# Rows of x to columns through a scratch in HBM and VectorE's 32x32 blocks, with f units in front of o units

## The chip, the cores and the metric

One Trainium2 chip (trn2), one core of it. The metric is the device time of one execution in microseconds, as the median of several runs; a profiled execution of the same kernel is taken beside them.

## The reference, cut to what matters

x and ctx are 32 batches of 256 rows of 512 numbers, all float32. Each batch gets a causal attention with 16 heads of 32 numbers, whose queries come from the normalised rows of x and whose keys and values come from ctx, and then a linear layer on rows quantised to a grid of 6-bit numbers.

```python
x = x + tanh(g_xattn[0]) * xattn(layernorm(x), ctx, ctx, w_q, b_q, w_k, b_k, w_v, b_v, w_o, b_o)
x = x + tanh(g_ffn[0]) * ffn(layernorm(x), weight, bias)
```

## The kernel before, in words

**Tiling.** Every product runs over columns that must lie on partitions, so rows of x, of ctx and of the quantised input have to be turned. Numbers are split in a high and a low part of type float32r, and a product is three matmuls (`three`, L546: hi by hi, hi by lo, lo by hi). A batch is two halves of 128 rows. Work comes in units: cT, xT and dT are turns of a half (rows of context, of normalised x, of the quantised rows), q and k are projections of a half of the heads, v, o and f of a half of the rows. q, k, v, o, f have four parts of three or six matmuls each, cT, xT and dT one part of four transposes. A unit takes one of four banks (`proj`) in turn.

**Steps and slots.** The program has 36 steps of 16 slots. Step i works at once on several batches: the context of batch i is loaded and turned; q half 0, k and v are of batch i-1; q half 1, the 16 heads' scores, maxima, exponentials and divisions are of batch i-2; o is of batch i-3 and f of batch i-4. One slot holds one head: TensorE makes its scores (L605, L606), turns the probabilities of the head three slots back (`transpose_probs`, L616, which waits for `div_ok`, the division by GpSimd), weighs values in slots 3 and 11 (L632), and then makes the parts of units that UNITS and SLOT_PARTS give to the slot. The scores of head h wait until VectorE has the maxima of head h-2 (`max_ok`).

**The engines.** Each engine runs its own program in order. VectorE per slot: maxima of the head (`maxima`, L891), reciprocal of the one before (L949), then what a unit finished in the slot before needs (`unit`: L920 for q_lo and k_lo, L943 for the low part of a turned half, L929 and L905 for o, L937 for f), a copy of the turned probabilities in every second slot (L1028), then xn (`normal_rows`, L1008, slots 1 and 3), oT_lo (L954), the steps of the quantisation (L966, L972, L979), the turns of context (`turn`, L998, slots 5 and 8), and the moments of x (slot 14). ScalarE: `unit` (q_hi and k_hi L758, aT_hi L772, vs L750), oT_hi, copies, exponentials (L735), cT_hi (L783). GpSimd: cT_lo (L498), divisions (L458), add of biases, powers, scaling.

**How rows are turned before.** Context (but for batch 0) is loaded in four DMAs of one quadrant of 32 partitions each into c_quads (`context`, L370) so that VectorE's 32x32 block transposes finish the turn in SBUF (cols); ScalarE and GpSimd split it. The normalised rows xn are turned by TensorE: 4 transposes a half (L660, kind xT), then ScalarE (L772) and VectorE (L943) read the bank.

**The DMA queue.** All DMAs are issued by SyncE (SP), in the order of its `step` (L389 to L435). A stack (`stack`, L374 to L382) is 12 DMAs that copy q_hi, q_lo, q_hi or k_hi, k_hi, k_lo of half the heads into q_stack or k_stack. The order of a step i is: k stack of pair 1 of batch i-2; loads of context i; load of x of batch i; q stack of pair 1 of batch i-2; stores of batch i-4; k stack of pair 0 of batch i-1; q stack of pair 0 of batch i-1 (waits for q_lo, `left["q"]`). There is one k_hi for all batches, so the first k unit of a batch may write it only when the last stack of k of the batch before has landed:

```python
                    if some(n := b + half):
                        for e in range(2):
                            act.wait_ge(stacked[kind][1 - half][e], STACK_DMAS * 16 * n)
```

In the first steps, at the start, TensorE turns the identity 12 times (WAKING, L543) before the context of batch 0 (L660) and the first weight (L582, `transpose_weight`).

Of the kernel before, what the change touches and what calls it, by code (L numbers as in the profile page):

```python
# [24 lines left out]
F32 = mybir.dt.float32  # L25
# [7 lines left out]
P = 128  # L33
# [32 lines left out]
WEIGHT_SLOTS = {"k": (1, (0, 0, 0, 0)), "q": (1, (4, 4, 4, 4)), "v": (1, (6, 9, 9, 9)), "o": (1, (10, 12, 12, 13)),  # L66
# [6 lines left out]
XB_SLOTS = (5, 6)  # L73
LN1_SLOT = SLOTS - 2
XN_SLOTS = (1, 3)
QUAD = 32
TURN_SLOTS = (5, 8)
TURN_SLOTS_1 = (12, 13)
# [4 lines left out]
def fused_kernel(nc, x, ctx_in, g_xattn, g_ffn, w_q, b_q, w_k, b_k, w_v, b_v, w_o, b_o, w_f, b_f, out):  # L83
# [16 lines left out]

    usual = [(u, part) for u, (kind, _, _) in enumerate(UNITS) for part in range(PARTS[kind])]
    slot_of = [s for s in range(SLOTS) for _ in range(SLOT_PARTS[s])]
    assert len(usual) == len(slot_of)
    lag_of = {(kind, half): lag for kind, half, lag in UNITS}
# [3 lines left out]
    for i in range(STEPS):  # L108
        if i == B + 2:

            for s, (kind, half) in LAST_O:
                work.setdefault((i, s), []).extend((kind, half, i - lag_of[kind, half], p) for p in range(PARTS[kind]))
        else:
            for (u, part), s in zip(usual, slot_of):
                kind, half, lag = UNITS[u]
                if live(i - lag):
                    work.setdefault((i, s), []).append((kind, half, i - lag, part))

    work[1, 0] = [("cT", half, 0, 0) for half in range(T)] + work.get((1, 0), [])

# [13 lines left out]
    def some(n):  # L134

        return not isinstance(n, int) or n > 0

    with ExitStack() as es:
# [29 lines left out]
        xn = sb("xn", [P, T, D])  # L168
        aT_hi = sb("aT_hi", [P, KC, S], F32R)
# [83 lines left out]
        turned = sem("turned")  # L253
# [64 lines left out]
        def turn_slots(b):  # L318

            return TURN_SLOTS_1 if b == 1 else TURN_SLOTS if b > 1 else ()  # L320
# [19 lines left out]
        def _(sp):  # L340
# [26 lines left out]
            def context(b):  # L367

                for g in range(NQ):
                    sp.dma_start(c_quads[g * QUAD:(g + 1) * QUAD, :, :],  # L370
                                 ctx_in[b, :, g * P:(g + 1) * P].rearrange("(n l) d -> l n d", l=QUAD)).then_inc(
                                     c_in, 16)
# [11 lines left out]
            def step(i, ph):  # L384
                if live(i - 2):

                    if some(n := HEADS * (i - 2)):

                        sp.wait_ge(max_ok, n)  # L389
                    sp.wait_ge(left["k"], 2 * (i - 2) + 2)  # L390
                    stack("k", i - 2, 1)
                if at(i, 0):
                    load_first()
                elif live(i):

                    if i == 1:
                        sp.wait_ge(done["cT"], 2)
                    else:  # L400
                        sp.wait_ge(turned, 2 * (i - 1))
                    context(i)

                    if i == 1:
# [18 lines left out]
                b = i - 1  # L423
                if live(b):
                    if some(b):


                        sp.wait_ge(max_ok, HEADS * (b - 1) + HEADS // 2)
                    else:

                        sp.wait_ge(left["k"], 2 * b + 1)
# [10 lines left out]
        def _(pool):  # L442
# [57 lines left out]

            def step(i, ph):
# [9 lines left out]
                for s in range(SLOTS):  # L511

                    for t, turn_slot in enumerate(turn_slots(i)):
                        if s == turn_slot + 2 and live(i):
                            context_lo(i, t)
                    lag, h = (2, s - 1) if s else (3, SLOTS - 1)
# [10 lines left out]
                    if i == 0 and s == LN1_SLOT + 1:  # L527
                        deviation_in(0)
                    if s == 0 and i > 1 and live(i - 1):
                        deviation_in(i - 1)  # L530
# [8 lines left out]
        def _(pe):  # L539
# [3 lines left out]
            for _ in range(WAKING):  # L543
# [20 lines left out]
            def transpose_weight(u, w, c):  # L564

                if w == "f" and c == 0:

                    pe.wait_ge(wd_ok, 1)
                elif w in "kv" and c == 0:
# [3 lines left out]
                elif w in "qo" and c % 2 == 0:  # L573
# [6 lines left out]
                cols = slice(c, D, KC) if w in "kv" else slice(c * P, (c + 1) * P)  # L580
# [58 lines left out]
            def unit(kind, half, b, part):  # L639
# [7 lines left out]
                if kind in ("xT", "cT", "dT"):  # L647
# [10 lines left out]
                    for c in range(KC):  # L658
                        cols = slice(c, D, KC) if kind == "cT" else slice(c * P, (c + 1) * P)
# [52 lines left out]
        def _(act):  # L712
# [27 lines left out]
            def unit(kind, half, b):  # L740
# [20 lines left out]
                else:  # L761
                    dst = cT_hi[:, 0] if kind == "cT" else aT_hi
                    if kind == "cT":
                        pass
                    elif kind == "xT":

                        if some(n := 2 * (b - 3) + half + 1):
                            act.wait_ge(done["f"], n)
                    else:
# [6 lines left out]
            def context_hi(b, t):  # L776

                act.wait_ge(turned, 2 * (b - 1) + t + 1)
                if some(n := 2 * (b - 1)):
# [4 lines left out]
                                     ACT.Copy).then_inc(hi_ok["cT"], 1)  # L784

# [17 lines left out]
            def step(i, ph):  # L803
                for s in range(SLOTS):
# [16 lines left out]
                    for t, turn_slot in enumerate(turn_slots(i)):  # L821
                        if s == turn_slot + 1 and live(i):
                            context_hi(i, t)
                    for chunk in weight_chunks(i, s - 1):
# [15 lines left out]
        def _(dve):  # L840
# [146 lines left out]
            def moments_in(b):  # L987

                dve.wait_ge(x_in, 16 * (b + 1))
                moments(b + 1, (0, 1), xs[:, b % X_RING], stats1, mom1, var1, st1, mo1, va1)  # L990

            def turn(b, t):

                dve.wait_ge(c_in, 16 + 16 * NQ * b)
                if b > 1:

                    dve.wait_ge(left["cT"], 2 * (b - 1) + t + 1)
                nc.vector.transpose(cols[:, t, :, :].rearrange("p c (n l) -> p n c l", l=QUAD),  # L998
                                    c_quads[:, t * NQ:(t + 1) * NQ, :].rearrange("p n (e c) -> p n c e",
                                                                                c=KC)).then_inc(turned, 1)  # L1000

            def normal_rows(b, t):

                dve.wait_ge(rs1, b + 1)
                if some(n := 2 * b):

                    dve.wait_ge(done["xT"], n)
# [3 lines left out]
            def step(i, ph):  # L1011
                for s in range(SLOTS):
# [16 lines left out]
                    if s in XN_SLOTS and i > 1 and live(i - 1):  # L1029
                        normal_rows(i - 1, XN_SLOTS.index(s))  # L1030
# [7 lines left out]
                    for t, turn_slot in enumerate(turn_slots(i)):  # L1038
                        if s == turn_slot and live(i):
                            turn(i, t)  # L1040
# [8 lines left out]
                    if s == LN1_SLOT and i > 1 and live(i):  # L1049
                        moments_in(i)  # L1050
                    if i == 1 and s == 1:
                        moments_in(0)
# [28 lines left out]
```

## Time and profile before

| what | value |
|---|---|
| median of 3 runs | 1389.93 us (1389.61 to 1392.1) |
| the profiled execution's own time | 1392.38 us |
| its span, first to last instruction | 1390.6 us |
| mean granted TensorE clock | 0.989 of full speed |
| TensorE matmuls busy | 1354.2 us, 97% |
| VectorE | 1124.7 us, 81% |
| ScalarE | 916.6 us, 66% |
| GpSimd | 938.7 us, 68% |
| DMA | 159.10 MB, 114 GB/s on average |

Busy time is the time in which an instruction runs; matmuls overlap in the pipeline, so that what one costs is the distance of its start from the next one's start and not its duration. The same holds, by 0.1 us or so, for VectorE. A row of the timeline begins with its start in us, then its duration (of all, where it ends with a count over x1), engine, line, operation, output and inputs; brackets at its end hold the idle time in front of it and what ended it.

### The profile page before, as it was taken

How to read it: one execution, taken by the hardware profiler on the slowest of the kernel's cores; microseconds unless marked ns; L12 is line 12 of the kernel's file. 1: busy time of each engine (PE TensorE's matmuls, PEld its weight loads, DVE VectorE, ACT ScalarE, POOL GpSimd, SP SyncE). 2: the span in 40 equal slices, each digit the busy share in tenths (PEclk: the TensorE clock that was granted, in tenths of full speed). 3: DMA queues.
4: the chain of work that ended last, by engine and by line, in shares of the span. 5: the costliest groups of instructions: out<-in, count | busy, mean ns of one | idle time of the engine just before them, and what ended most of it. 6: DMA issues, size and time to landing. Idle time of an engine off the chain costs nothing.

```text
span 1390.6 us, 34895 instructions
## 1 busy us (share of the span) xinstructions
PE 1354.2 (97%) x10608; PEld 1198.5 (86%) x10608; DVE 1124.7 (81%) x4219; ACT 916.6 (66%) x2969; POOL 938.7 (68%) x1449
## 2 busy tenths in 40 slices
PE   7899999999999999999999999999999999999987
PEld 7788888898888888888888888888888889889865
DVE  5768888788888888888878878888888888888773
ACT  4667666667666666667666667666666666766661
POOL 1657776677676777676677676677677667767564
PEclk9999999999999999999999999999999999999998
DMA  8444344444444444434444434444444444443320
GB/s 253 118 112 107 103 111 124 118 129 107 109 109 120 124 128 117 107 101 119 121 126 123 108 99 115 126 119 124 110 106 109 126 118 128 110 116 99 88 62 31
DMA packets 181912, 159.10 MB, mean 114 GB/s; under 512 B 30176, under 2 KB 164320, under 8 KB 181728
## 3 DMA queue, kind: packets, MB, share of 16 engines
q1 hardware_dynamic: 181728, 156.88, 43.3%
q8 instruction: 87, 1.43, 0.5%
q14 instruction: 97, 0.79, 0.2%
HBM read 39.33 MB, written 16.78 MB: 40 GB/s over the span
## 4 chain that ended last, share of the span: by engine, by line
PE 59%; DVE 20%; SPq 9%; issue 5%; DMA 3%; ACT 1%; POOL 1%; DVEq 0%; ACTq 0%; POOLq 0%
PE proj L549 14%; PE proj L551 13%; PE proj L550 13%; SPq L380 9%; PE pT_ps L616 8%; DVE all_probs L891 5%; PE proj L632 3%; DMA k_stack<-k_lo 3%; DVE stats L899 3%; PE s_ps L605 3%; PE proj L660 2%; DVE all_probs L1028 2%; DVE k_lo L920 2%; PE s_ps L606 1%; DVE oT_lo L954 1%
## 5 line engine op out<-in xcount | busy, mean ns | idle before, releaser
L458 POOL TENSOR_TENSOR all_probs<-all_probs,rden 128x128 f32<-128x128 f32 (+1 forms) x1024 | 504.1, 514 | 347.5 <-DVE rden L949 346.5
L735 ACT ACTIVATE all_probs<-all_probs,neg_max 128x128 f32<-128x128 f32 (+1 forms) x1024 | 458.3, 449 | 242.4 <-DVE neg_max L891 242.2
L891 DVE CUSTOM_DVE_ANT_0 all_probs<-s_ps,causal 128x128 f32<-128x128 f32 (+1 forms) x1024 | 324.4, 354 | 144.2 <-PE s_ps L606 137.1
L616 PE MATMUL pT_ps<-ident,all_probs 128*128 128x128 f32 x1536 | 265.0, 282 | 9.9 <-POOL all_probs L458 7.2
L735 ACT ACTIVATION_READ_ACCUMULATOR all_probs<-all_probs,neg_max 128x1 f32 x1024 | 193.1, 189 | 0.0
L817 ACT ACTIVATE all_probs<-pT_ps 128x384 f32<-128x384 f32 x256 | 125.4, 490 | 87.4 <-PE pT_ps L616 87.2
L616 PEld LDWEIGHTS pT_ps<-ident,all_probs 128*128 128x128 f32 x1536 | 160.8, 142 | 25.2 <-issue 14.1
L549 PE MATMUL proj<-cT_hi,wk_hi 128*128 128x256 f32 x512 | 153.8, 300 | 1.4 <-DVE wk_lo L844 1.4
L605 PE MATMUL s_ps<-k_stack,q_stack 96*128 96x256 f32 x512 | 152.8, 299 | 2.1 <-DVE neg_max L891 2.0
L549 PE MATMUL proj<-aT_hi,wq_hi 128*128 128x256 f32 x512 | 151.0, 295 | 2.3 <-DVE aT_lo L943 2.3
L550 PE MATMUL proj<-cT_lo,wk_hi 128*128 128x256 f32 x512 | 142.7, 279 | 0.0
L551 PE MATMUL proj<-cT_hi,wk_lo 128*128 128x256 f32 x512 | 142.5, 278 | 0.0
L550 PE MATMUL proj<-aT_lo,wq_hi 128*128 128x256 f32 x512 | 142.4, 278 | 0.0
L551 PE MATMUL proj<-aT_hi,wq_lo 128*128 128x256 f32 x512 | 142.4, 278 | 0.0
L1028 DVE COPY all_probs<-pT_ps 128x384 f32<-128x384 f32 x256 | 139.7, 546 | 2.1 <-PE pT_ps L616 1.9
L549 PE MATMUL proj<-wf_hi,aT_hi 128*128 128x512 f32 x256 | 111.9, 437 | 6.6 <-DVE oT_lo L954 5.8
L606 PE MATMUL s_ps<-k_stack,q_stack 96*128 96x128 f32 x512 | 116.1, 227 | 0.0
L549 PE MATMUL proj<-wo_hi,oT_hi 128*128 128x512 f32 x260 | 110.9, 426 | 0.9 <-DVE oT_lo L954 0.9
L758 ACT ACTIVATE k_hi<-proj,bias_k 128x256 fp32r<-128x256 f32 x128 | 53.0, 464 | 85.6 <-DMA k_stack<-k_lo 81.0
L605 PEld LDWEIGHTS s_ps<-k_stack,q_stack 96*128 96x128 f32 x512 | 96.9, 189 | 14.3 <-DVE neg_max L891 3.3
L549 PE MATMUL proj<-wv_hi,cT_hi 128*128 128x512 f32 x256 | 108.3, 423 | 0.0
L606 PEld LDWEIGHTS s_ps<-k_stack,q_stack 96*128 96x128 f32 x512 | 98.2, 192 | 10.5
(119 smaller groups left out, 3607.9 us busy)
## 6 DMA issues: line engine op xcount, KB each, us to landing
k_stack<-k_hi SPq DMA_DIRECT2D x512, 64.0 KB, 2.0
q_stack<-q_hi SPq DMA_DIRECT2D x512, 64.0 KB, 2.1
xs_yz<-in_x SPq DMA_DIRECT2D x32, 512.0 KB, 5.2
k_stack<-k_lo SPq DMA_DIRECT2D x256, 64.0 KB, 2.0
q_stack<-q_lo SPq DMA_DIRECT2D x256, 64.0 KB, 2.1
out<-xs_yz SPq DMA_DIRECT2D x64, 256.0 KB, 2.3
c_quads<-in_ctx SPq DMA_DIRECT2D x124, 128.0 KB, 2.9
vs<-in_L_xattn_w_k SPq DMA_DIRECT2D x2, 512.0 KB, 5.8
```

Source lines behind the costliest of these rows:

```text
L380: sp.dma_start(dst[r * DK:(r + 1) * DK, h:h + GROUP + 1:GROUP, :].bitcast(F32), src[j * DK:(j + 1) * DK, :, :].bitcast(F32)).then_inc(stac ...
L458: last = nc.gpsimd.tensor_tensor(p, p, rden[:, sd, t, h:h + 1].to_broadcast([P, (1 + t) * P]), ALU.mult)
L549: nc.tensor.matmul(out, a_hi(c), b_hi(c), start=c == 0, stop=False)
L550: nc.tensor.matmul(out, a_hi(c), b_lo(c), start=False, stop=False)
L551: last = nc.tensor.matmul(out, a_lo(c), b_hi(c), start=False, stop=c == KC - 1)
L605: nc.tensor.matmul(bank[:, P:3 * P], q_stack[:, h, P:S], k_stack[:, h, :], start=True, stop=True)
L606: nc.tensor.matmul(bank[:, 0:P], q_stack[:, h, 0:P], k_stack[:, h, 0:P], start=True, stop=True).then_inc(s_done, 1)
L616: last = nc.tensor.transpose(pT_ps[h % 2][:, m * P:(m + 1) * P], probs[:, h % P_RING, m * P:(m + 1) * P], ident[:, :])
L735: last = nc.scalar.activation(probs[:, h % P_RING, cols], probs[:, h % P_RING, cols], ACT.Exp, scale=-1.0, bias=neg_max[:, sd, t, h:h + 1] ...
L817: nc.scalar.activation(probsT[:, h % AV_HEADS, :], pT_ps[1][:, 0:3 * P], ACT.Copy).then_inc(pT_odd, 1)
L891: last = nc.vector.tensor_tensor_reduce(probs[:, h % P_RING, cols], s_ps[h % 2][:, cols], causal[:, (1 - t) * P:], 1.0, MASKED, ALU.add, A ...
L1028: nc.vector.tensor_copy(probsT[:, h % AV_HEADS, :], pT_ps[0][:, 0:3 * P]).then_inc(pT_even, 1)
```

## The change

xT leaves TensorE for all batches but the first. The normalised rows xn (now made in slot 14 of step i for batch i, after moments in slots 7 and 9 and the power in slot 11) are written to a scratch in HBM, xn_rows, by one DMA (`rows_out`), and read back by four DMAs in quadrants (`rows_back`) into the same place in SBUF. VectorE turns them in 32x32 blocks in slots 5 and 6 into cols, halves swapped, ScalarE makes aT_hi and GpSimd aT_lo (`rows_hi`, `rows_lo`). The turns of context move to slots 0 and 1 and their loads to the end of the step before. The order of parts is written out in SLOT_WORK: f comes in front of o, and q half 0 ends in slot 12 (before: slot 10). The weight of q is turned with the stride c, D, KC like k and v. The identity is turned another 16 times before the first weight.

```diff
-UNITS = [("q", 1, 2), ("dT", 0, 4), ("k", 0, 1), ("dT", 1, 4), ("f", 0, 4), ("xT", 0, 1), ("f", 1, 4), ("xT", 1, 1),
-         ("o", 0, 3), ("o", 1, 3), ("q", 0, 1), ("v", 0, 1), ("k", 1, 1), ("v", 1, 1)]
-SLOT_PARTS = (3, 3, 3, 1, 3, 4, 3, 3, 3, 3, 3, 1, 3, 3, 3, 2)
+SLOT_WORK = ("q1 q1 q1", "dT0 q1 k0", "k0 k0 k0", "dT1", "f0 f0 f0", "f0 f1 f1", "f1 f1 o0", "o0 o0 o0", "o1 o1 o1",
+             "o1 v0 v0", "v0 v0", "q0", "q0 q0 q0", "k1 k1 k1", "k1 v1 v1", "v1 v1")
-WAKING = 12
+WAKING = (12, 16)
-XB_SLOTS = (5, 6)
-LN1_SLOT = SLOTS - 2
-XN_SLOTS = (1, 3)
+XB_SLOTS = (4, 5)
+LN1_SLOTS = (7, 9)
+RSTD_SLOT = 11
+XN_SLOT = 14
-TURN_SLOTS = (5, 8)
-TURN_SLOTS_1 = (12, 13)
+C_TURNS, C_TURNS_1, C_TURNS_2 = (0, 1), (12, 13), (2, 3)
+X_TURNS = (5, 6)
...
     work[1, 0] = [("cT", half, 0, 0) for half in range(T)] + work.get((1, 0), [])
+    work[1, 5] = [("xT", half, 0, 0) for half in range(T)] + work.get((1, 5), [])
+    xn_rows = nc.dram_tensor("xn_rows", [S, D], F32, kind="Internal").ap()
+        xn_quads = xn[:, :, :].rearrange("p t (n d) -> p (t n) d", d=P)
...
+            def rows_out(b):
+                sp.wait_ge(xn_ok, T * (b + 1))
+                sp.dma_start(xn_rows.rearrange("(t p) d -> p t d", p=P), xn[:, :, :]).then_inc(xn_out, 16)
+
+            def rows_back(b):
+                sp.wait_ge(xn_out, 16 * b)
+                for quadrant, rows in quarters(xn_rows):
+                    sp.dma_start(xn_quads[quadrant, :, :], rows).then_inc(xq_in, 16)
...
             def step(i, ph):
+                if i > 1 and live(i - 1):
+                    rows_out(i - 1)
                 if live(i - 2):
...
                     sp.wait_ge(left["k"], 2 * (i - 2) + 2)
                     stack("k", i - 2, 1)
...
                     sp.dma_start(xs[:, place(ph, 0), :, :], batch_of(x, i)).then_inc(x_in, 16)
+                if i > 1 and live(i - 1):
+                    rows_back(i - 1)
                 if live(i - 2):
...
                     stack("q", i - 2, 1)
+                b = i - 1
+                if live(b):
+                    if some(b):
+                        sp.wait_ge(max_ok, HEADS * (b - 1) + HEADS // 2)
+                    sp.wait_ge(left["k"], 2 * b + 1)
+                    stack("k", b, 0)
                 if live(i - 4):
...
                 if live(b):
-                    stack("k", b, 0)
                     sp.wait_ge(left["q"], 2 * b + 1)
                     stack("q", b, 0)
+                if i > 0 and live(i + 1):
+                    context(i + 1)
...
+            def rows_lo(b, t):
+                pool.wait_ge(hi_ok["xT"], 2 * b + t + 1)
+                tok = slice(t * P, (t + 1) * P)
+                nc.gpsimd.tensor_tensor(aT_lo[:, :, tok], cols[:, 1 - t, :, :], aT_hi[:, :, tok].bitcast(F32),
+                                        ALU.subtract).then_inc(left["xT"], 1)
...
+            def turn_rows(b, t):
+                dve.wait_ge(xq_in, 16 * NQ * b)
+                if live(b + 1):
+                    dve.wait_ge(left["cT"], T * (b + 1) + T - t)
+                else:
+                    dve.wait_ge(left["xT"], T * (b - 1) + t + 1)
+                turn(xn_quads, t, 1 - t, x_turned)
```

## Rows read from the trace of the kernel before

**Rows 1.** Windows view, 600 to 641.3: stretch, length, busy time by engine, clock, DMA

```profile
600.00:641.30 41.30, 41.30 (x332) 36.78 (x331) 35.18 (x132) 28.56 (x95) 29.54 (x47) 1.00 0.44 117
```

**Rows 2.** Timeline of the SyncE queue, three stretches: start, duration, what is issued

```profile
162.11 1.22 SPq L380 DMA_DIRECT2D k_stack<-k_hi  x2
...
616.49 1.23 SPq L380 DMA_DIRECT2D k_stack<-k_hi  x2
...
624.16 2.08 SPq L370 DMA_DIRECT2D c_quads<-in_ctx  x4
626.28 0.45 SPq L412 DMA_DIRECT2D xs_yz<-in_x  x1
627.07 0.59 SPq L380 DMA_DIRECT2D q_stack<-q_hi  x1
...
635.43 1.18 SPq L421 DMA_DIRECT2D out<-xs_yz  x2
...
1236.86 1.23 SPq L380 DMA_DIRECT2D k_stack<-k_hi  x2
```

**Rows 3.** Waits view, whole span: us in total, times, longest

```profile
ACT k_hi L758 <- DMA k_stack<-k_lo: 81.0, 30, 3.4
```

**Rows 4.** Timeline of ScalarE, the first k unit of a step

```profile
625.61 0.84 ACT L758 ACTIVATE k_hi<-proj,bias_k 128x256 fp32r<-128x256 f32 x2 [1.95 <-DMA k_stack<-k_lo]
```

**Rows 5.** VectorE: timeline, end of q half 0; waits view, 625.6 to 647.8

```profile
646.55 0.85 DVE L920 SCALAR_TENSOR_TENSOR q_lo<-proj,bias_q,q_hi 128x256 fp32r<-128x256 f32 x2
...
DVE all_probs L891 <- PE s_ps L606: 1.9, 4, 0.9
```

**Rows 6.** Timeline of TensorE around one xT unit

```profile
629.98 0.39 PE L551 MATMUL proj<-wf_hi,aT_lo 128*128 128x512 f32 x1
630.21 0.60 PE L660 MATMUL proj<-ident,xn 128*128 128x128 f32 x4
...
630.88 0.39 PE L550 MATMUL proj<-wf_lo,aT_hi 128*128 128x512 f32 x1
```

**Rows 7.** Groups by line and form: busy us, mean ns; idle before, releaser

```profile
L943 DVE TENSOR_TENSOR aT_lo<-proj,aT_hi 128x512 fp32r<-128x512 f32 x128 | 86.8, 678 | 5.6 <-ACT aT_hi L772 5.6
...
L998 DVE STREAM_TRANSPOSE cols<-c_quads 128x512 f32<-128x512 f32 x62 | 68.0, 1098 | 0.0
...
L498 POOL TENSOR_TENSOR cT_lo<-cols,cT_hi 128x512 fp32r<-128x512 f32 x62 | 81.0, 1307 | 0.5 <-ACT cT_hi L783 0.5
```

**Rows 8.** Timeline of VectorE: starts, from which spacings are taken

```profile
606.81 0.67 DVE L972 TENSOR_REDUCE amax<-xs_yz 128x16 f32<-128x512 f32 x1
607.40 0.53 DVE L966 TENSOR_SCALAR xs_yz<-xs_yz,mom,rstd 128x512 f32<-128x512 f32 x1
...
611.09 0.54 DVE L1028 COPY all_probs<-pT_ps 128x384 f32<-128x384 f32 x1
611.54 0.17 DVE L979 TENSOR_SCALAR blk<-amax 128x16 f32<-128x16 f32 x1
...
612.33 0.29 DVE L891 CUSTOM_DVE_ANT_0 all_probs<-s_ps,causal 128x128 f32<-128x128 f32 x1
...
612.97 1.27 DVE L899 BATCH_NORM_STATS2 stats<-xs_yz 128x6 f32<-128x512 f32 x2
...
614.62 0.17 DVE L909 TENSOR_SCALAR var<-mom 128x2 f32<-128x2 f32 x1
```

**Rows 9.** Timeline of GpSimd: the division of head 3

```profile
629.00 0.97 POOL L458 TENSOR_TENSOR all_probs<-all_probs,rden 128x128 f32<-128x128 f32 x2 [2.85 <-DVE rden L949]
```

**Rows 10.** Timeline of TensorE: scores of two slots in a row

```profile
606.61 0.28 PE L605 MATMUL s_ps<-k_stack,q_stack 96*128 96x256 f32 x1
...
609.22 0.28 PE L605 MATMUL s_ps<-k_stack,q_stack 96*128 96x256 f32 x1
```

**Rows 11.** Timeline of TensorE at the start: the first weight's transposes

```profile
8.64 1.95 PE L582 MATMUL s_ps<-ident,vs 128*128 128x128 f32 x8 [2.13 <-DMA vs<-in_L_xattn_w_k]
```

**Rows 12.** Windows view, 60 to 64, columns as in rows 1

```profile
60.00:64.00 4.00, 1.34 (x8) 1.20 (x7) 3.55 (x14) 2.86 (x12) 3.99 (x7) 0.79 0.38 95
```

More of the change, by code:

```diff
@@ L99, in live @@
         return not isinstance(b, int) or 0 <= b < B
[L101 to L104, printed above, removed]
+    usual = [(s, (name[:-1], int(name[-1]))) for s in range(SLOTS) for name in SLOT_WORK[s].split()]
+    assert all(sum(unit == u for _, u in usual) == PARTS[unit[0]] for unit in LAGS)
     work = {}
@@ L111, in fused_kernel @@
             for s, (kind, half) in LAST_O:
-                work.setdefault((i, s), []).extend((kind, half, i - lag_of[kind, half], p) for p in range(PARTS[kind]))
+                work.setdefault((i, s), []).extend((kind, half, i - LAGS[kind, half], p) for p in range(PARTS[kind]))
         else:
[L114 to L117, printed above, removed]
+            part_of = dict.fromkeys(LAGS, 0)
+            for s, unit in usual:
+                if live(i - LAGS[unit]):
+                    work.setdefault((i, s), []).append((*unit, i - LAGS[unit], part_of[unit]))
+                part_of[unit] += 1
     work[1, 0] = [("cT", half, 0, 0) for half in range(T)] + work.get((1, 0), [])
+    work[1, 5] = [("xT", half, 0, 0) for half in range(T)] + work.get((1, 5), [])
     taken = []
@@ L398, in step @@
                     if i == 1:
[L399 to L404, printed above, removed]
+                        context(1)
                         sp.wait_ge(xn_ok, 2)
@@ L541, in _ @@
             pe.wait_ge(ident_ok, 1)
-            for _ in range(WAKING):
+            for _ in range(WAKING[0]):
                 nc.tensor.transpose(proj[BANKS - 1][:, 0:P], ident[:, :], ident[:, :])
@@ L762, in unit @@
                     dst = cT_hi[:, 0] if kind == "cT" else aT_hi
[L763 to L769, printed above, removed]
+                    if kind == "dT":
                         act.wait_ge(done["q"], 2 * (min(b + 2, B - 1) if isinstance(b, int) else b + 2) + 2)
@@ L985, in scales, with moments_in @@
                                         ALU.mult).then_inc(inv_ok, 1)
-            def moments_in(b):
+            def moments_in(b, t):
                 dve.wait_ge(x_in, 16 * (b + 1))
-                moments(b + 1, (0, 1), xs[:, b % X_RING], stats1, mom1, var1, st1, mo1, va1)
-            def turn(b, t):
-                dve.wait_ge(c_in, 16 + 16 * NQ * b)
[L995 to L1000, printed above, removed]
+                nc.vector.bn_stats(stats1[:, t, :], xs[:, b % X_RING, t, :]).then_inc(st1, 1)
+                if t == T - 1:
+                    dve.wait_ge(st1, T * (b + 1))
+                    for n in range(T):
+                        last = nc.vector.bn_aggr(mom1[:, n, :], stats1[:, n, :])
+                    last.then_inc(mo1, 1)
+                    dve.wait_ge(mo1, b + 1)
+                    nc.vector.tensor_scalar(var1[:, :], mom1[:, :, 1], LN_EPS, None, ALU.add).then_inc(va1, 1)
@@ new lines, in turn, with turn_context @@
+            def turn(quads, t, place, turned):
+                nc.vector.transpose(cols[:, place, :, :].rearrange("p c (n l) -> p n c l", l=QUAD),
+                                    quads[:, t * NQ:(t + 1) * NQ, :].rearrange("p n (e c) -> p n c e",
+                                                                              c=KC)).then_inc(turned, 1)
+            def turn_context(b, t):
+                dve.wait_ge(c_in, 16 + 16 * NQ * b)
+                if b > 2:
+                    dve.wait_ge(left["xT"], T * (b - 2) + T - t)
+                elif b == 2:
+                    dve.wait_ge(left["cT"], T * (b - 1) + t + 1)
+                turn(c_quads, t, t, c_turned)
@@ L1028, in step @@
                         nc.vector.tensor_copy(probsT[:, h % AV_HEADS, :], pT_ps[0][:, 0:3 * P]).then_inc(pT_even, 1)
-                    if s in XN_SLOTS and i > 1 and live(i - 1):
-                        normal_rows(i - 1, XN_SLOTS.index(s))
+                    if s == XN_SLOT and i > 0 and live(i):
+                        for t in range(T):
+                            normal_rows(i, t)
                     for r in range(2):
```

96 lines of the change are left out of this document (61 added, 35 removed).

## The prediction

> **What bounds the kernel now.** I read the windows view first. In the stretch [rows 1] TensorE is busy 41.30 of 41.30 us at full granted clock, VectorE 35.18, GpSimd 29.54, ScalarE 28.56: TensorE sets the time. A step takes 41.34 us: between the first and the last of these SyncE rows, 26 steps apart, lie 1074.75 us [rows 2]. The other thing to see is in the same group: SyncE's own queue. A stack of q or k rows is 12 DMAs, and the next item of the queue starts 7.67 us (616.49 to 624.16) or 8.36 us (627.07 to 635.43) later. Four stacks, four loads of context, one of x and two stores are some 36 us of issue in 41.34. What hangs on that queue stands in the waits view [rows 3]: ScalarE waits 30 times, 81.0 us in all, to overwrite k_hi until the k stack of the batch before has landed, and by the code SyncE's q stack waits for q_lo in turn. So beside TensorE there is a ring, once per step. Call K the start of k_hi for k half 0 (625.61, 1.5 us after the last of the k stack's DMAs left SyncE [rows 4]) and Q the end of q_lo for q half 0 (646.55 plus 0.85, 647.40 [rows 5]). From K to Q are 21.8 us of VectorE, TensorE and ScalarE; from Q to the next K SyncE issues two stacks. Two fast stacks are 15.3 us and the landing 1.5, so today's ring has up to 41.3 - 21.8 - 15.3 - 1.5 = 2.7 us of slack, and TensorE stays full.
>
> **The change, part by part.**
>
> *TensorE, less work.* A unit of four transposes sits between two matmuls: from 629.98 to 630.88 are 0.90 us where two matmul spacings of 0.23 would be 0.46 [rows 6]. 0.44 us a unit, two units a step, 31 steps: 27.3 us, all on today's bound. TensorE alone would take 40.46 a step.
>
> *VectorE.* Off: two subtractions of 678 ns; on: two 32x32 turns of 1098 ns [rows 7], 0.84 us a step more, 36.0 of 40.5. Not a bound by its sum. ScalarE reads cols where it read a bank: nothing counted, it is busy 28.56 of 41.30. GpSimd gains two subtractions like cT_lo's, 1307 ns [rows 7], 32.2 of 40.5; hidden by its idle time, and I place them behind divisions that TensorE wants only later.
>
> *SyncE.* On: one store of 512 KB to the scratch, which I take at 0.5 us of issue (the 512 KB load of x takes 0.45 [rows 2]; between 0.4 and 1.1), and four loads shaped like the context's, 2.1 us. The sum becomes 38.7. But what counts is where things now stand: q half 0 is finished by TensorE in slot 12, not slot 10; then come its stack, the four context loads (formerly behind the k stack), the new store, and only then the k stack whose landing ScalarE waits for at slot 3. The loads of context, now issued from Q+7.7 on, land about 11.5 after Q, and VectorE's first turn of context (slot 0) waits for them some 5 us; it still reaches slot 3 at about Q+17.7, ahead of k_lo at Q+21, so that wait is covered by the ring, for as long as the ring is this long. The wait of rows_back for the store is covered: the k stack lies between. The wait for max_ok before the k stack of pair 0 also finds slack, since SyncE then waits for Q anyway.
>
> *The ring after the change, Q to K.* Stack of q 8.0 (mean of 7.67 and 8.36), context 2.1, store 0.5, stack of k 8.0, landing 1.5: 20.1 us, with 19.4 to 22 as ends (every issue fast; both slow and a landing 1 us longer).
>
> *The ring, K to Q.* Of the 21.8 us before, VectorE idles 1.9 in front of scores [rows 5], so 19.9 are work. The stretch now ends in slot 13 instead of 11. It gains, in spacings of starts [rows 8]: two pairs of maxima with reciprocal at 0.64, a copy of probabilities 0.45, both block maxima 1.18, a second normalise 0.46 (as long as the copy), one scales 0.79, the moments of x 1.8, oT_lo of the other half 0.59 (an instruction of the block maximum's 0.67 us). It loses one xn (0.46, moved to slot 14) and the two subtractions (1.18). Both turns were in it already. Together plus 4.9: 24.8 us of VectorE without a pause. TensorE's way through the same stretch: head 3 is divided 4.36 us after K (629.00 and 0.97 [rows 9]), 3.9 without the xn in front, so slot 6 starts at K+3.7; from there to slot 13 are five full slots of 2.6 us (606.61 to 609.22 [rows 10]), one of 1.9 and one of 2.8, so 17.7, then maxima and q_lo 1.7: 23.1. VectorE's 24.8 is the later one.
>
> *Sum per step.* 24.8 + 20.1 = 44.9, plus 0.4 for the clock (below): 45.3 us, 3.96 more than 41.34. TensorE's 0.88 us saving buys nothing, for it is no longer the bound: it will wait in slot 6 for the division of head 3, which waits for ScalarE's k_hi.
>
> *Sum over the kernel.* 27 steps (4 to 30) at 3.96 are 106.9. Steps 31 and 32 have no context load left to issue, so 1.8 each, 3.7. Steps 2 and 3 lack the o or f work and are slower than TensorE's sum already; I give them 4 together. The tail stays.
>
> *Start.* 16 turns of the identity before the first weight. Today TensorE idles 2.13 us until the weight lands at 8.64, and eight transposes take 1.95 us with their tail, at the lower clock [rows 11]. Sixteen take 3.4 us, so the weight's transposes begin 1.1 us later; if the clock is then up (2.4 instead of 1.2 GHz), the 40 instructions behind cost half, some 3 us less. Between -3 and +1; I take -1.5.
>
> Total: +106.9 + 3.7 + 4 - 1.5 = +113. The profiled execution took 1392.4 us (span 1390.6), 2.5 above the median of 1389.9; so 1505 against that execution and 1503 against the median.
>
> **A rule weighed here.** The rows say that a DMA's issue occupies SyncE for about 0.64 us in a stretch of 12, and that an engine ends up waiting for the last of them. The Trainium skill, "DMA: Bandwidth & Descriptors", "Issuing engines are not separate DMA queues", says that the sequencer's time to start a DMA is usually small against the DMA itself. By that rule the order on SyncE would be almost free, and the sum would be the first rival's. The trace disagrees for DMAs of this size: 0.64 us of issue each, against 1.5 us from the end of the last issue to its landing.
>
> **Rivals.**
>
> *1. Faster: the queue does not bind and TensorE's saving comes through.* The mechanism is 62 units fewer on an engine that has no idle time: 1389.9 - 27.3 - 1.5 = 1361. It decides if the ring takes less than 40.5 us, 4.4 below my sum; for that, SyncE would have to issue stacks in some 6 us instead of 8, or k_hi would have to be free without its landing. For it: TensorE has no idle time in the stretch now. Against it: even the fast ends, 23.1 and 19.4, make 42.5. Chance 0.10, and 0.02 that the two effects cancel.
>
> *2. The ring with TensorE's way as its middle part.* If VectorE's 24.8 is overcounted, 23.1 + 19.5 = 42.6 a step, 1.3 more than before: 27 x 1.3, and -0.5 each in steps 31 and 32, +3 for steps 2 and 3, -1.5: about 1425. Chance 0.15.
>
> *3. The ring and the clock.* Once TensorE waits some 2 us at slot 0 (first half of the q stack lands 5.4 after Q, three us late) and again at slot 6, the clock may fall each time. In the stretch 60 to 64, with TensorE busy 1.34 of 4 us, the mean granted clock is 0.79 [rows 12], partly at 1.2 GHz. Seven us at half clock cost 3.5: TensorE's way becomes 26.6 and overtakes VectorE's 24.8. With 20.1 to 21 for the rest, 47.2 a step: 27 x 5.9 + 8 + 5 - 1.5 = +171, 1561. Against it: the gaps are short, and full work follows. The Trainium skill, "TensorE: Matmul & The Clock Gate", "HAM oscillation", describes a loop whose waits for DMAs let the clock fall in every pass, which is this case's pattern; whether 2 us are enough, no row here shows for a full step. Chance 0.18; its milder half is the 0.4 us in my sum.
>
> *4. The rows come back late.* rows_back is issued behind 512 KB of x. If it lands after K+5.0, where VectorE's slot 5 asks for it, each us of lateness is a us of the ring. It is at about that point; 0 to 1 us, inside the range.
>
> **The numbers.** Forecast (44 to 46.5 a step) 0.55, rival 3 0.18, rival 2 0.15, faster 0.10, no change 0.02. The time is that of the likeliest, 1503. The range reaches from rival 2 to rival 3, 1425 to 1560, and leaves out the faster case and the far end of the clock. A measurement here tells 0.2% from no change. Faster 0.10, same 0.02, slower 0.88.
>
> **What the changed profile would show.** The four transposes of xn only in step 1; TensorE's share falls from 97% to about 90, with idle time in front of the probabilities' transposes released by GpSimd. ScalarE still waits at k_hi for k_stack, some 3 us or more each, and VectorE's wait for the loads of context in slot 0 is new. SyncE waits for q_lo some 5 us or more a step and never for k_lo; the k stack of pair 1 starts some 10.6 us after q_lo. VectorE has no pause from k_lo in slot 3 to q_lo in slot 13. The clock after each gap tells rival 3. The forecast is wrong if ScalarE no longer waits at k_hi, or if a step takes 40.5 us with TensorE full.

## The result: 1595.4 us, 14.8% slower

The changed kernel takes 1595.4 us (median of 4 runs, 1591.38 to 1598.6) beside 1390.6 us for the kernel before on the same chip: ratio 1.1477, 95% interval [1.1459, 1.1495]. The direction was forecast; the time was not, since 1595 lies above the range of 1425 to 1560. The profiled execution's span is 1594.2 us against 1390.6.

The head of the profile of after: TensorE's share fell from 97% to 88%.

```profile
span 1594.2 us, 34649 instructions
...
PE 1408.2 (88%) x10376; PEld 1223.1 (77%) x10376; DVE 1143.3 (72%) x4219; ACT 913.5 (57%) x2969; POOL 1011.9 (63%) x1511
...
PE 50%; SPq 21%; DVE 10%; issue 10%; DMA 7%; POOL 1%; ACT 0%; DVEq 0%; POOLq 0%; ACTq 0%
SPq L404 17%; PE proj L581 10%; PE proj L582 10%; PE proj L583 10%; PE pT_ps L652 8%; PE proj L668 7%; DMA c_quads<-in_ctx 5%; SPq L387 3%; DVE all_probs L936 3%; PE s_ps L641 2%; DVE q_lo L965 2%; PE proj L696 2%; DVE all_probs L1099 1%; PE s_ps L642 1%; DMA xn<-xn_rows 1%
```

The last two lines are the chain that ended last. SyncE's queue (SPq), which an engine-by-engine sum never shows, holds a fifth of it; 17% of 1594 us is 271 us, 9 per step, which is one stack and a little. A chain that went through two stacks a step, as the forecast's ring does, would hold nearly twice that. The transfers in it are those of context, not those of k_stack.

The waits view of after, us in total, times, longest, agrees (the third line answers to [rows 3]):

```profile
DVE cols L1048 <- DMA c_quads<-in_ctx: 180.8, 29, 7.2
...
PE proj L668 <- issue: 80.5, 32, 2.7
...
ACT k_hi L794 <- DMA k_stack<-k_lo: 52.3, 30, 6.2
```

ScalarE waits less for the k stack than before (52.3 against 81.0 us), and VectorE waits for the loads of context in 29 steps, 6.2 us each. The windows view of one step of after, columns as in [rows 1]:

```profile
600.00:647.30 47.30, 42.54 (x321) 37.04 (x320) 35.29 (x135) 28.01 (x93) 32.22 (x48) 0.93 0.49 125
```

VectorE has nearly the 35.2 us of before and TensorE 42.54 us, in a step of 47.3: no engine is a bound by its sum.

**Where the time went.** SyncE issues the store to xn_rows once a step, 31 times, the first at 60.2 and the last at 1480.2: 47.33 us a step, 5.99 more than the 41.34 of before. The first k stack of step 2 is issued at 60.72 where before it was at 40.45: 20.3 us at the start. The same stack of step 32 follows at 1480.84 where before it was at 1278.52, so the 30 steps between cost 182.0 us (a little over 30 x 5.99, as the first steps of before are shorter than 41.34). The remaining 1.3 of the 203.6 us of span lie in the last steps.

**One steady step.** The chain through it, in order of time: start, duration, what.

```profile
615.67 0.40 DVE q_lo L965
616.09 0.59 SPq L404
...
623.12 0.60 SPq L404
623.76 1.52 SPq L387
...
626.31 2.93 DMA c_quads<-in_ctx
629.33 0.32 issue
...
630.95 0.46 DVE all_probs L1099
631.41 2.68 issue
634.10 2.79 PE proj L668 x32
636.88 0.83 PE pT_ps L652 x3
...
663.44 0.59 SPq L404
```

It begins and ends with the same event, SyncE's first issue of the q stack after q half 0 is done. q_lo ends at 616.07 (Q). SyncE issues 12 DMAs of the stack until 623.72 and four of context until 626.76, the last lands at 629.24 (626.31 plus 2.93): 13.2 after Q. Only then can VectorE go on, and the timeline of the three other engines shows who stands behind it:

```profile
629.26 1.08 DVE L1048 STREAM_TRANSPOSE cols<-c_quads 128x512 f32<-128x512 f32 x1 [6.54 <-DMA c_quads<-in_ctx]
...
630.91 0.40 ACT L771 ACTIVATE all_probs<-all_probs,neg_max 128x128 f32<-128x128 f32 x1 [7.24 <-DVE neg_max L936]
...
634.10 2.79 PE L668 MATMUL proj<-all_probs,vs 128*32 128x256 f32 x32 [2.72 <-issue]
...
636.91 0.84 ACT L794 ACTIVATE k_hi<-proj,bias_k 128x256 fp32r<-128x256 f32 x2 [1.53 <-DMA k_stack<-k_lo]
...
637.79 0.88 DVE L965 SCALAR_TENSOR_TENSOR k_lo<-proj,bias_k,k_hi 128x256 fp32r<-128x256 f32 x2 [2.63 <-ACT k_hi L794]
```

The turn of context stands in VectorE's slot 0, in front of the maxima of head 1. ScalarE's exponential of head 1 waits 7.24 us for those, and behind it in ScalarE's program are cT_hi, aT_hi, q_hi and then the copy of the last head's turned probabilities of the batch before (L858, at 633.51). TensorE needs that copy for the values in slot 3 (L668), which start at 634.10, as the copy ends; the profile has only "issue" for this wait, and the time of the copy is what names it. From there TensorE has no gap until it has made q half 0 in slot 12; q_lo ends at 663.42. So: Q to landing 13.2, landing to values 4.8, values to the next Q 29.3: 47.3 us. k_hi starts at 636.91, after TensorE is already running again, and holds nobody up but VectorE for 2.63 us.

### The profile page after: what moved, and what is told of

It reads as the page before. It is cut to its first block, busy times and chain, and to the rows that moved or that the text cites. A ratio compares the mean times of both kernels' runs of the same rounds, so it can differ in the third digit from the quotient of the medians.

```text
span 1594.2 us, 34649 instructions
## 1 busy us (share of the span) xinstructions
PE 1408.2 (88%) x10376; PEld 1223.1 (77%) x10376; DVE 1143.3 (72%) x4219; ACT 913.5 (57%) x2969; POOL 1011.9 (63%) x1511
## 4 chain that ended last, share of the span: by engine, by line
PE 50%; SPq 21%; DVE 10%; issue 10%; DMA 7%; POOL 1%; ACT 0%; DVEq 0%; POOLq 0%; ACTq 0%
SPq L404 17%; PE proj L581 10%; PE proj L582 10%; PE proj L583 10%; PE pT_ps L652 8%; PE proj L668 7%; DMA c_quads<-in_ctx 5%; SPq L387 3%; DVE all_probs L936 3%; PE s_ps L641 2%; DVE q_lo L965 2%; PE proj L696 2%; DVE all_probs L1099 1%; PE s_ps L642 1%; DMA xn<-xn_rows 1%
## 5 line engine op out<-in xcount | busy, mean ns | idle before, releaser
L652 PE MATMUL pT_ps<-ident,all_probs 128*128 128x128 f32 x1536 | 281.8, 296 | 17.0 <-POOL all_probs L479 10.2
L641 PE MATMUL s_ps<-k_stack,q_stack 96*128 96x256 f32 x512 | 161.8, 316 | 56.1 <-DVE neg_max L936 43.8
L668 PE MATMUL proj<-all_probs,vs 128*32 128x256 f32 (+1 forms) x2048 | 134.8, 421 | 80.5 <-issue 80.5
L652 PEld LDWEIGHTS pT_ps<-ident,all_probs 128*128 128x128 f32 x1536 | 170.3, 149 | 38.1 <-issue 24.8
L1048 DVE STREAM_TRANSPOSE cols<-c_quads 128x512 f32<-128x512 f32 x62 | 67.7, 1091 | 180.8 <-DMA c_quads<-in_ctx 180.8
L858 ACT ACTIVATE all_probs<-pT_ps 128x384 f32<-128x384 f32 x256 | 125.1, 489 | 103.5 <-PE pT_ps L652 102.9
L668 PEld LDWEIGHTS proj<-all_probs,vs 128*32 128x32 f32 x2048 | 77.6, 137 | 122.6 <-issue 108.6
L641 PEld LDWEIGHTS s_ps<-k_stack,q_stack 96*128 96x128 f32 x512 | 101.0, 197 | 86.6 <-DVE neg_max L936 50.6
L581 PE MATMUL proj<-aT_hi,wq_hi 128*128 128x256 f32 x512 | 153.5, 300 | 0.0
L581 PE MATMUL proj<-cT_hi,wk_hi 128*128 128x256 f32 x512 | 150.4, 294 | 1.8 <-DVE wk_lo L889 1.8
L965 DVE SCALAR_TENSOR_TENSOR k_lo<-proj,bias_k,k_hi 128x256 fp32r<-128x256 f32 x128 | 55.4, 474 | 83.5 <-ACT k_hi L794 83.5
```

The source lines that it names most:

```text
L581: nc.tensor.matmul(out, a_hi(c), b_hi(c), start=c == 0, stop=False)
L641: nc.tensor.matmul(bank[:, P:3 * P], q_stack[:, h, P:S], k_stack[:, h, :], start=True, stop=True)
L652: last = nc.tensor.transpose(pT_ps[h % 2][:, m * P:(m + 1) * P], probs[:, h % P_RING, m * P:(m + 1) * P], ident[:, :])
L668: last = nc.tensor.matmul(bank[j * DK:(j + 1) * DK, half * S + kt * P:(half + 1) * S], vs[:, sd, kt, d:d + DK], probsT[:, GROUP * half + j ...
```

## Experiments

Step lengths below are taken as above, from the first and the last of the 31 issues of the store to xn_rows. Diffs are against the changed kernel unless said otherwise. Theory A is the context ring just read. Its rivals name something else: SyncE's order as such, the ring over k_hi, the clock.

### ctx_early: context in front of the q stack

```diff
+                if i > 1 and live(i + 1):
+                    context(i + 1)
                 if live(b):
                     sp.wait_ge(left["q"], 2 * b + 1)
                     stack("q", b, 0)
-                if i > 0 and live(i + 1):
+                if i == 1:
                     context(i + 1)
```

> The changed kernel with the loads of context i+1 issued by SyncE in front of the q stack of pair 0 (from step 2 on), not behind it. Theory A (the context ring): the step of 47.3 us is set by q_lo, q stack 7.7, context loads and their landing 5.5, VectorE's first context turn (waited 6.5 us), ScalarE's copy of head 15 behind it, and TensorE's values in slot 3. Then the wait at the context turn goes, and what is left is the ring over the k stack: 17.9 us from q_lo to k_hi and 24.8 of VectorE, 42.8 a step with the clock full again, so 27 steps less by 4.5, some 120 us: about 1473. Theory B (the k stack's ring as predicted, with the clock as its excess): only the 2.1 us of issue leave the ring, 1595 - 58 = about 1535, and ScalarE's wait at k_hi stays.

1514.87 us, ratio 1.0884 [1.0826, 1.0942]; span 1509.6, 44.41 a step (stores from 61.7 to 1394.1). The wait for context is gone from the waits view, and the one of the forecast's ring has taken its place:

```profile
ACT k_hi L796 <- DMA k_stack<-k_lo: 149.6, 31, 6.6
...
PE pT_ps L654 <- DVE all_probs L1101: 77.9, 31, 4.4
```

In one step of its timeline (ScalarE, TensorE, VectorE) Q is at 629.20 and the next at 673.46:

```profile
647.78 0.84 ACT L796 ACTIVATE k_hi<-proj,bias_k 128x256 fp32r<-128x256 f32 x2 [4.61 <-DMA k_stack<-k_lo]
...
650.15 0.52 PE L654 MATMUL pT_ps<-ident,all_probs 128*128 128x128 f32 x3 [2.23 <-DVE all_probs L1101]
...
653.88 1.11 DVE L1050 STREAM_TRANSPOSE cols<-xn 128x512 f32<-128x512 f32 x1 [0.98 <-DMA xn<-xn_rows]
```

Q to K is 18.6 (the forecast's 20.1 without 2.1 of context is 18.0), K to Q 25.7 (forecast 24.8, plus the late rows of rival 4: 0.98). So the forecast's ring exists and is about as long as forecast, but it is the second one. The gain is 2.9 us a step and not A's 4.5, since A's figure had this ring too short. The time alone decides nothing: it lies 42 us above A's and 20 us below B's. The waits do, and they are A's.

### turn_late: the turn of context two slots later

```diff
-C_TURNS, C_TURNS_1, C_TURNS_2 = (0, 1), (12, 13), (2, 3)
+C_TURNS, C_TURNS_1, C_TURNS_2 = (2, 3), (12, 13), (2, 3)
```

> The changed kernel with one edit: VectorE turns the context in slots 2 and 3 of every step instead of 0 and 1. SyncE's order and the work of every engine stay. Theory A (the step of 47.33 us is the ring q_lo, q stack, landing of the context loads, VectorE's turn of context in slot 0, ScalarE's exponential and copy behind it, values in slot 3, q half 0 in slot 12): the wait moves behind two more heads, some 5 us, and mostly goes; the ring over k_hi is next, about 44.4 us a step as with the context loads early, perhaps 1 us more because the turn of xn in slot 5 then waits for GpSimd's low part of context. 44.4 to 45.5 a step, about 1505 to 1540 us. Theory B (the late landing or SyncE's order itself holds the step, whoever waits for it): no gain, 1585 to 1605 us.

1619.1 us, ratio 1.1649 [1.163, 1.1669]; span 1616.3, 47.97 a step. That is a miss for A's number, and it isn't B either, by the timeline of a step (VectorE, then ScalarE, then TensorE):

```profile
642.20 1.16 DVE L1048 STREAM_TRANSPOSE cols<-c_quads 128x512 f32<-128x512 f32 x1 [0.27 <-DMA c_quads<-in_ctx]
...
657.00 1.11 DVE L1048 STREAM_TRANSPOSE cols<-xn 128x512 f32<-128x512 f32 x1 [1.37 <-POOL cT_lo L519]
...
649.52 0.84 ACT L794 ACTIVATE k_hi<-proj,bias_k 128x256 fp32r<-128x256 f32 x2 [8.02 <-DMA k_stack<-k_lo]
...
651.88 0.87 PE L652 MATMUL pT_ps<-ident,all_probs 128*128 128x128 f32 x3 [4.50 <-DVE all_probs L1099]
```

The wait for context is 0.27 us: that ring is open. The ring over k_hi closes instead, with 8.02 us of waiting: Q (628.75) to K 20.8, K to the next Q (676.70) 27.2. Against ctx_early each part is longer for a reason in the rows: in Q to K the four context loads, 3.19 us in this step, still stand in front of the k stack; in K to Q, TensorE starts again after a gap of 4.50 us at half clock (windows view, 652 to 656, the column behind the busy times):

```profile
652.00:656.00 4.00, 3.93 (x11) 2.75 (x12) 3.63 (x14) 3.47 (x12) 3.67 (x5) 0.50 1.01 187
```

Nearly 4 us at half clock are 2 us of work lost; K to Q is 1.5 us longer than in ctx_early. The two rings of the changed kernel are thus almost equal, and opening one alone leaves the step to the other.

### qfirst_only: q half 0 two slots earlier

```diff
-             "o1 v0 v0", "v0 v0", "q0", "q0 q0 q0", ...
+             "o1 q0 q0", "q0 q0", "v0", "v0 v0 v0", ...
```

> The changed kernel with one edit: the parts of q half 0 in slots 9 and 10 in front of v half 0. Loads of context stay behind the q stack, the moments of batch 1 stay early. Theory A (both rings start at q_lo, so that its slot decides): in steps of 40.5 us q_lo now ends some 10.3 us before slot 0 instead of 5, the loads of context land 13.2 after it, VectorE's first context turn waits 2 us instead of 6.5, and the copy of head 15 comes just in time: 40.5 to 41.5 a step, and with the start unchanged 1385 to 1420. Theory B: the place of the loads behind the stack costs by itself, 43 us a step or more, over 1450.

1442.04 us, ratio 1.0381 [1.0337, 1.0426]; span 1440.7, 42.44 a step (53.2 to 1326.5). This edit touches neither SyncE's order nor a wait; it shortens what both rings have in common. By one step of the timeline (SyncE, VectorE, TensorE, and VectorE again), Q is at 639.49:

```profile
647.71 2.09 SPq L387 DMA_DIRECT2D c_quads<-in_ctx  x4
...
652.27 1.11 DVE L1048 STREAM_TRANSPOSE cols<-c_quads 128x512 f32<-128x512 f32 x1 [2.71 <-DMA c_quads<-in_ctx]
...
657.14 1.51 PE L668 MATMUL proj<-all_probs,vs 128*32 128x256 f32 x32 [0.93 <-issue]
...
680.26 0.86 DVE L965 SCALAR_TENSOR_TENSOR q_lo<-proj,bias_q,q_hi 128x256 fp32r<-128x256 f32 x2
```

Q to turn 12.8, turn to values 4.9, values to the next Q 24.0, where it was 29.3 (41.6 in this step; the mean is 42.44). The two slots left out were 5.4 us of TensorE in after (scores of slots 11 and 13, 655.80 and 661.18), and at a clock of 1.00 behind the values 1.3 more are gone; VectorE gives 1.6 of it back, since q_lo now comes 3.0 us behind TensorE's scores of its slot (677.24) and not 1.4. The ring is still the limit, 2 us above TensorE's 40.5, which is why A's 1420 was missed by 22 us. Of the 153.5 us of span gained, 147 are steps (30 times 4.89) and 7 the start, where q half 0 of step 1 is earlier too.

### ctx_qfirst and ctx_mom_qfirst: the edits together

ctx_qfirst has the two edits above, context in front of the q stack and q half 0 earlier:

> The changed kernel with two edits: the context loads in front of the q stack, and q half 0 in slots 9 and 10; the moments of batch 1 stay in slots 7 and 9 of step 1. Theory A (both rings fall below TensorE's sum, and the start is a price of its own): a step of 40.5 as with all three edits, and a start about 11 us later than there (the first store of rows at 53.2 instead of 41.8): 1383 to 1390 us. Theory B (the moments also hold back every step, or the start's price is hidden behind the rings): 1372 or over 1400 us.

1383.97 us, ratio 0.996 [0.9944, 0.9976]; stores from 53.7 to 1267.3, 40.45 a step. A's numbers, 40.5 and 1383 to 1390, hold. ctx_mom_qfirst adds the later moments of the next section:

> Both edits (context loads in front of the q stack; moments of batch 1 in slot 11 of step 1) and the parts of q half 0 in slots 9 and 10 in front of v half 0, so that q_lo comes two slots earlier. Theory A (two rings, nothing else): q_lo to k_hi stays 17.9 us and k_hi to q_lo falls from 24.8 to about 21 us, 39 a step, below TensorE's own 40.5: TensorE is the bound again without the 62 units, about 1390 - 27 = 1363, and no more than 1375. Theory B: the rows come back from the scratch too late, or SyncE's own sum (38.7 of 40.5 us) keeps it from this: 42 a step or more, over 1420.

1372.98 us, ratio 0.9865 [0.9836, 0.9893]; 40.53 a step, first store at 41.8, and in the windows view of 600 to 900 TensorE has 299.39 busy us of 300 at clock 1.00. Repeated as best_again:

> The version with the three edits once more, for an interval beside the other two: 1373, some 18 us below the kernel before, and 40.5 us a step. If the earlier time was chance, it lies above 1380.

1372.17 us, ratio 0.9875 [0.9821, 0.9928]. So this version takes 1.3% less than the kernel before, a small gain, but with the 95% interval below 1 in both runs, and 14% less than the changed one. The mechanism is that of the forecast's first rival, reached with other orders: a step of 40.5 where TensorE alone was to take 40.46. Its 1361 isn't reached: the first k stack of step 2 is issued at 43.92, 3.5 us later than before and not 1.5 earlier, and the 30 steps behind it save 22 us where the forecast has 27 in 31 steps (before, these 30 have 41.27 us on average).

### mom_late: the start

```diff
-                    if s in LN1_SLOTS and i > 0 and live(i):
+                    if s in LN1_SLOTS and i > 1 and live(i):
                         moments_in(i, LN1_SLOTS.index(s))
+                    if i == 1 and s == RSTD_SLOT:
+                        for t in range(T):
+                            moments_in(1, t)
```

> The changed kernel with the moments of x of batch 1 taken in slot 11 of step 1, not in slots 7 and 9; all other steps as they are. Theory A: TensorE's gap of 20 us at the start comes from VectorE, which waits 10.1 us in slot 7 of step 1 for x of batch 1 while the parts of the v weight are due behind it; then the first k stack of step 2 starts near 43 instead of 60.7 us and the time falls by 12 to 20 us, to about 1578. Theory B: the gap comes from the late load of the weights (18 MB are asked for at once and the DMA engines are full until 30 us), so another wait takes its place and the time falls by less than 5.

1582.95 us, ratio 1.1373 [1.134, 1.1406]: 12 us less than the changed kernel, with the same 47.36 a step and the first store at 47.8. What it takes away stands in the timeline of after, VectorE and then TensorE:

```profile
30.68 0.69 DVE L1035 BATCH_NORM_STATS2 stats<-xs_yz 128x6 f32<-128x512 f32 x1 [10.09 <-DMA xs_yz<-in_x]
...
40.65 0.77 PE L581 MATMUL proj<-wv_hi,cT_hi 128*128 128x512 f32 x1 [20.45 <-issue]
```

VectorE stands 10.09 us in slot 7 of step 1 in front of x of batch 1, whose load SyncE issues only at 21.25, behind its wait for the weight of o; the load lands 9.4 us later, while the DMA engines are full (DMA share 1.11 from 20 to 30 us). The last two parts of wv_lo (39.28 to 40.55) are behind that wait in VectorE's program, and TensorE waits 20.45 us until they are there. With the edit TensorE's gap is 5.93 us and ends at 27.57 instead of 40.65. The 18 MB of theory B are not in the record: by the windows view of after 8.4 MB move in the first 30 us.

best_xfirst takes the version with all three edits and issues that load in front of the wait for the weight of o:

```diff
+                sp.wait_ge(xn_ok, 2)
+                sp.dma_start(xs[:, 1, :, :], batch_of(x, 1)).then_inc(x_in, 16)
                 sp.wait_ge(wT_done, KC * (WEIGHTS.index("q") + 1))
                 load_weight("o")
...
-                        sp.wait_ge(xn_ok, 2)
...
+                    if i > 1:
+                        sp.dma_start(xs[:, place(ph, 0), :, :], batch_of(x, i)).then_inc(x_in, 16)
```

> The version with all three edits (context loads early, moments of batch 1 late, q half 0 first) and the load of x of batch 1 issued before SyncE waits for the weight of o. VectorE's wait of 4.1 us for x of batch 1 should go. Theory A: it is on the path of the start, 2 to 4 us less than 1373. Theory B: the DMA engines are full there, so what x gains the loads behind it lose, within 1 us.

1372.28 us, ratio 0.9876 [0.9838, 0.9915]: no gain over 1372.17, as in theory B. VectorE's wait of 4.08 us for x is gone from the timeline; TensorE waits 3.00 us for the weight of o instead, and VectorE 2.04 us for context.

before_wake puts the second set of 16 turns of the identity, and nothing else of the change, into the kernel before:

```diff
             def transpose_weight(u, w, c):
+                if u == 0:
+                    for _ in range(16):
+                        nc.tensor.transpose(proj[BANKS - 1][:, 0:P], ident[:, :], ident[:, :])
```

> The kernel before with nothing but 16 more turns of the identity in front of the first weight. The prediction's term: between -3 and +1 us, taken as -1.5. Seen in the trace: the first weight's transposes start at 9.7 instead of 8.6, and the clock is at 2.4 GHz for the k unit. The rival: no gain, because the start is bound by the arrival of other weights.

1389.23 us, ratio 0.9987 [0.9974, 1.0], so a gain isn't clear of none. The timeline answers to [rows 11]: eight transposes of the weight take 1.13 us instead of 1.95, and the first product of k starts at 12.67 instead of 13.71. The sixteen turns take 2.51 us and not 3.4, so the weight's transposes start at 8.81, hardly later than before.

```profile
6.46 2.51 PE L568 MATMUL proj<-ident 128*128 128x128 f32 x16
8.81 1.13 PE L585 MATMUL s_ps<-ident,vs 128*128 128x128 f32 x8
...
12.67 0.38 PE L549 MATMUL proj<-cT_hi,wk_hi 128*128 128x256 f32 x1 [1.75 <-DVE wk_lo L847]
```

### after_fill: the clock

Eighteen idle turns of the identity in front of the scores of slot 3 and 24 behind them, in steps 3 to 32, fill most of TensorE's gap:

```diff
+            def filler(n, b):
+                free_bank("av", 1, b)
+                for _ in range(n):
+                    nc.tensor.transpose(bank_of("av", 1, b)[:, 0:P], ident[:, :], ident[:, :])
...
                 for s in range(SLOTS):
+                    if s == 3 and 2 < i < B + 1:
+                        filler(18, i - 3)
                     if live(i - 2):
                         scores(i - 2, s)
+                    if s == 3 and 2 < i < B + 1:
+                        filler(24, i - 3)
```

> The changed kernel with idle TensorE work in its two gaps of a step: 18 turns of the identity in front of the scores of slot 3 and 24 behind them, into a bank that nobody reads then; they compute nothing that is used. Theory A (the clock is part of the step): a step of 47.3 us holds some 2.4 us of work at half clock after the gap; with the gaps filled the granted clock stays near 1.00 and the step falls to about 45, 1595 - 29 x 2.4 = about 1525. Theory B (the clock falls but its loss is hidden by VectorE, whose chain is as long): the clock comes back and the step stays at 47, over 1575.

1560.29 us, ratio 1.1227 [1.1163, 1.1292]; 46.08 a step, 1.25 less, though TensorE does more. First two windows of after around the gap, then two of after_fill at the same place of a step:

```profile
632.00:636.00 4.00, 1.90 (x24) 1.33 (x28) 3.12 (x14) 3.38 (x10) 3.93 (x5) 0.50 0.40 98
636.00:640.00 4.00, 4.00 (x33) 3.20 (x23) 2.21 (x9) 3.08 (x10) 1.83 (x4) 0.73 0.88 222
```

```profile
612.00:616.00 4.00, 4.00 (x38) 4.00 (x37) 2.98 (x8) 1.31 (x5) 1.19 (x3) 1.00 0.67 207
616.00:620.00 4.00, 4.00 (x57) 3.29 (x56) 2.92 (x14) 3.18 (x10) 3.96 (x5) 1.00 0.41 99
```

After the gap the changed kernel's values run at 1.2 GHz (32 matmuls take 2.79 us, 1.51 in after_fill). So the clock is worth at least 1.25 us of the 6.0 that a step lost, half of A's guess. It is at least that because the turns can hold up the values themselves, as in one step of after_fill (ScalarE's copy, then TensorE):

```profile
617.29 0.49 ACT L867 ACTIVATE all_probs<-pT_ps 128x384 f32<-128x384 f32 x1
...
618.50 1.51 PE L673 MATMUL proj<-all_probs,vs 128*32 128x256 f32 x32
```

The copy ends at 617.78 and the values start 0.7 us later, as the last turn ends; from there to the next Q (646.31) are 27.8 us against 29.3 in after, 1.5 less. The wait for context stays, 176.9 us in 29 steps. The Trainium skill, "TensorE: Matmul & The Clock Gate", "HAM oscillation", describes a loop whose waits for DMAs let the clock fall in every pass; this trace agrees, and puts the price at some 1.3 to 1.5 us of 47.

## Why the prediction was right in sign and wrong in size

**What held.** TensorE alone at 40.46 a step: 40.45 and 40.53 measured once nothing else bound. That SyncE's order after the later q half 0 costs more than TensorE saves: yes. Q to K of 20.1: 20.8 in after (616.07 to 636.91). K to Q of 24.8: 25.7 in ctx_early. The price of SyncE's issue, about 0.64 us a DMA of a stack, stands in every chain. The first weight: the first product of k starts at 12.14 in after, 1.6 us earlier than before, of which before_wake shows 1.0; that these 1.5 us reach the end of the kernel isn't shown.

**The step that failed.** In the part on SyncE I had the right wait and dismissed it: VectorE's first turn of context "waits for them some 5 us; it still reaches slot 3 at about Q+17.7, ahead of k_lo at Q+21, so that wait is covered by the ring". I followed only VectorE from slot 0 to k_lo. TensorE has a way of its own out of that wait: exponential of head 1, ScalarE's copy, values in slot 3 at Q+18.0. It doesn't pass k_lo at all; behind it stand nine slots of TensorE's work until q half 0, 29.3 us. A wait on one engine is covered only if every engine that stands behind it is covered, and here the bound engine wasn't. Followed through with the landing as I had it (11.5) and TensorE's slots, the same sum gives 11.5 + 4.8 + 28.0 (29.3 without 1.3 of slow clock): some 44 us, about as long as my ring. So the missing path alone doesn't give 47.3: with my own terms on it the forecast would have come out about the same, and longer terms on it make the rest. These are the landing at Q+13.2, not 11.5, and the clock, 1.3 us or more against 0.4 in the sum. Of the landing, 0.9 us is the issue (the four took 3.00 us in this step against 2.08 in [rows 2]) and the rest was too short from the start: the profile of before gives a load of context 2.9 us from issue to landing, with which my sum would have had Q+12.2.

```profile
c_quads<-in_ctx SPq DMA_DIRECT2D x124, 128.0 KB, 2.9
```

The signs that I named were off in the same way. ScalarE's wait at k_hi was to be 3 us or more and is 52.3 us in 30 steps, 1.7 each; TensorE's idle time was to stand in front of the probabilities' transposes, released by GpSimd, and stands in front of the values and of the scores of slot 3.

**Rival 3** gave 47.2 a step, by another way: the ring over k_hi with a slow TensorE. The number is that of the measured step, the mechanism isn't: in after, TensorE runs again 2.8 us before K, and the clock gives back 1.3 to 1.5 us, not 3.5. That the number fits is luck. turn_late, though, is rival 3 as described: 20.8 and 27.2 with half clock behind the gap.

**The start** was the second miss: -1.5 forecast, +20.3 measured. I costed the moved moments only in the steady step. In step 1 they stand in front of the last parts of the weight of v, and wait for a load which that step issues late. Of the 20 us, mom_late gives back 12 (first store at 47.8 against 60.2); 7 come from q half 0's place (qfirst_only, 53.2 against 60.2); with both, the first store is at 41.8.

**Sum.** Measured 182.0 for the steps, 20.3 for the start and 1.3 for the end, 203.6 in all. Forecast 114.6 for the steps and -1.5 for the start. Of the 90.5 between them the steps have 67, the start 22.

**Open.** The parts f in front of o and the turned stride of the weight of q weren't tried by themselves. Both are in ctx_qfirst too, whose step is 40.45 us, so neither lengthens a steady step once the rings are short enough. Why the issue of the four context loads takes 2.09 us in some steps and 2.6 to 3.0 in others stays open.

## What to carry to other kernels

When an edit makes one engine wait in a place where it did not, list every engine that stands behind the waiting instruction in its own program and follow each to the end of the loop: the longest of these rings is the step, and two rings of nearly equal length are best cut by what they share (here: q half 0 two slots earlier, 4.9 us a step for no instruction). A moved operation is to be costed in the first pass of the loop as well, where its input may not have been asked for yet.

## What was not expected of the hardware

The issue of a DMA isn't of constant length: in 14 steps of after between 435 and 1055 us the four loads of context took 1.83 to 2.09 us nine times and 2.57 to 3.00 five times. In the step read here the first of them took 1.52 us and the others 0.45. The 124 single issues of these loads last 0.35 to 1.82 us, median 0.45.

TensorE's clock took gaps of different length differently: behind a gap of 2.23 us (ctx_early) it stayed at 2.4 GHz (granted 1.00 from 640 to 660), behind 4.50 (turn_late), and behind 1.72 and 2.72 in a row (after), it went to 1.2. In after the 32 matmuls of the values behind the gap take 2.79 us in step upon step, and 1.51 us with the gap filled. So a gap of TensorE cost its own length in one kernel, and some 1.3 to 1.5 us more in the other.
